# One Trainium2 core: the graph-attention walk in steps of two pairs, four of eight gathers made ahead, and coarser signals in the fill

## The reference

```
x += gat(layernorm(x))       # the part this case is about
x += moe_top1(layernorm(x))  # 8 experts, capacity 977
x += gcn2(layernorm(x))      # two graph convolutions over the same edges, with batch norm
x += moe_top2(layernorm(x))  # 8 experts, two per node

gat(h): feat = (h @ W) as [N, 4 heads, 64]
        el, er = <feat, attn_l>, <feat, attn_r> per head
        e = leaky_relu(el[src] + er[dst], 0.2)
        alpha = softmax of e over the edges of each dst
        out = elu(segment_sum(feat[src] * alpha, dst) + bias);  return h + out
```

## Time and profile before

| what | value |
|---|---|
| time, three runs | 7741.1 us median (7734.77 to 7762.5) |
| profiled execution: time, span | 7729.86 us, 7728.1 us |
| mean granted TensorE clock | 0.829 |
| busy: PE, PEld, DVE, ACT, POOL | 5449.5, 4407.3, 3508.0, 1732.1, 2142.1 us |
| fill: first and last product (line 607) | 327.7 and 2080.5 us |
| walk: first make_onehot (line 731) and last collect (line 772) | 2089.6 and 4025.1 us |
| indirect gathers (line 671) | 1664, busy 1674.6 us |

### The profile page before, as it was taken

How to read it: one execution, slowest core, us unless ns; L and a number is a source line. 1 busy time by engine, 2 the same in 40 slices (tenths; PEclk the granted TensorE clock), 3 DMA queues, 4 the chain that set the end, 5 groups by cost and what they waited for, 6 DMA issues and landing times. The chain is left out here.

```text
span 7728.1 us, 130980 instructions
## 1 busy us (share of the span) xinstructions
PE 5449.5 (71%) x37484; PEld 4407.3 (57%) x37485; DVE 3508.0 (45%) x10470; ACT 1732.1 (22%) x4193; POOL 2142.1 (28%) x2057
## 2 busy tenths in 40 slices
PE   2411115655577777777764995999969999549998
PEld 1200003333355555555543994888858888539997
DVE  5411117866666666666675555111161121532222
ACT  0200004666622222222222333000020000133332
POOL 2477770000055555555542220000000000052221
PEclk8655557877788888788875998999989999759999
DMA  3476661222244444444434662444402222336665
GB/s 119 121 212 195 193 202 58 92 86 98 101 116 116 118 116 116 116 115 116 117 91 135 177 177 75 157 152 157 158 26 102 96 95 92 121 136 181 183 180 169
DMA packets 448603, 1001.55 MB, mean 130 GB/s; under 512 B 56758, under 2 KB 314157, under 8 KB 428812
## 3 DMA queue, kind: packets, MB, share of 16 engines
q1 hardware_dynamic: 329116, 650.63, 26.1%
q0 software_dynamic: 112144, 268.88, 13.4%
q10 hardware_dynamic: 7200, 80.28, 2.5%
HBM read 713.64 MB, written 295.09 MB: 131 GB/s over the span
## 5 line engine op out<-in xcount | busy, mean ns | idle before, releaser
L671 POOL DMA_INDIRECT arena<-table,arena x1664 | 1674.6, 1006 | 2056.5 <-DVE arena L760 1623.9
L1249 PE MATMUL banks<-arena 128*128 128x256 bf16 x14700 | 1625.5, 273 | 25.5 <-DMA arena<-counts 25.5
L1249 PEld LDWEIGHTS banks<-arena 128*128 128x128 f16 x14700 | 1440.4, 98 | 206.7 <-DMA arena<-counts 26.3
L607 PE MATMUL banks<-arena 128*128 128x392 bf16 x2368 | 651.9, 436 | 1108.8 <-issue 718.8
L831 PE MATMUL banks<-arena 128*128 128x261 f32 x3328 | 1188.5, 489 | 162.0 <-DVE arena L760 81.3
L607 PEld LDWEIGHTS banks<-arena 128*128 128x128 bf16 x2368 | 350.1, 152 | 1410.1 <-issue 1373.4
L831 PEld LDWEIGHTS banks<-arena 128*128 128x128 f32 x3328 | 697.4, 233 | 276.4 <-DVE arena L760 93.6
L1868 POOL DMA_INDIRECT expert_in<-arena,slot x147 | 148.3, 1009 | 2306.2 <-DVEq L1809 2263.3
L1303 DVE TENSOR_TENSOR rings<-rings,banks 128x256 f32<-128x256 f32 x98 | 41.3, 421 | 1347.4 <-PE banks L1241 1347.4
L585 DVE TENSOR_TENSOR arena<-arena 128x1024 bf16<-128x1024 f16 x296 | 203.9, 689 | 988.5 <-remote 487.4
L2084 PEld LDWEIGHTS banks<-yt_ring,arena 128*128 128x128 f32 x5184 | 607.7, 193 | 15.4 <-DVE yt_ring L1973 4.1
(11 more groups left out here) (325 smaller groups left out, 5096.9 us busy)
## 6 DMA issues: line engine op xcount, KB each, us to landing
arena<-counts SPq DMA_DIRECT2D x100, 1568.0 KB, 6.6
arena<-in_L_ffn_W SPq DMA_DIRECT2D x114, 1024.0 KB, 5.2
edge_rows<-arena SPq DMA_DIRECT2D x312, 264.0 KB
arena<-edge_rows SPq DMA_DIRECT2D x312, 264.0 KB
counts<-arena ACTq DMA_DIRECT2D x50, 1568.0 KB, 5.1
arena<-in_L_ffn_w SPq DMA_DIRECT2D x64, 1024.0 KB
expert_in<-arena SPq DMA_DIRECT2D x25, 2028.0 KB
arena<-table,arena POOLq DMA_INDIRECT x1664
```

Source lines behind the costliest of these rows:

```text
L607: pe.matmul(psum_all[:, bass.ds(at_[p % 16], KEYS)], oh_b[:, p // LB % (OR // LB), :, p % LB], oh_k[:, p // KB % (OR // KB), :, p % KB], s ...
L671: pool.indirect_dma_start(out=got[:, u, j, :], out_offset=None, in_=table0, in_offset=bass.IndirectOffsetOnAxis(ap=src_sb[:, 2 * pair + j: ...
L1249: last = pe.matmul(psum[u][:, 0:D], a_ring[:, u, a, :], parts[:, a, k, :], start=(a == 0 and k == 0), stop=(a == NT - 1 and k == 2))
```

## The change

Everything is in the block described. In the fill, `hot` is raised every 8 steps instead of 4 and `done` every 4 instead of 1, with the numbers that others wait for scaled accordingly (`etab` is rounded up to whole groups of four); the number for `zeroed` now lies in the low bits of every fourth `ptab` entry, and TensorE takes it apart in registers instead of reading `ztab`. `KEPT` is 0, 1, 4, 5: four of eight, so that 416 pairs (832 gathers) are made ahead. The walk works on two pairs (q = 0 to 3) in each instruction where it can, and per q one signal takes the place of two. Per q TensorE does add_up(q), turn(q+3), spread(q+2); VectorE messages(q+1), score_sum(q+2), score_max(q+2), collect for the first pair, score_clamp(q+2), collect for the second, make_onehot(q+4); ScalarE copy_onehot(q+3), weights(q+2). A gather of q is four indirect DMAs behind one wait; a store or a load is one DMA of 512 rows. The diff, cut:

```diff
-KEPT = (0, 3, 6)
+KEPT = (0, 1, 4, 5)
+UQ = UN // 2
+KEPT_Q = tuple(u // 2 for u in KEPT[::2])
+LIVE_Q = tuple(u // 2 for u in LIVE[::2])
...
                     link(dve.tensor_scalar(ptab, ptab, 7, 9, ALU.bitwise_and, ALU.logical_shift_left))
+                    lead = ptab.rearrange("p (g u) -> p u g", u=PG)[:, 0, :]
+                    link(dve.tensor_tensor(lead, lead, ztab, ALU.add))
...
+                    link(dve.tensor_scalar(etab, etab, PG - 1, None, ALU.add))
+                    link(dve.tensor_scalar(etab, etab, PG.bit_length() - 1, None, ALU.arith_shift_right))
...
-                                    dve.wait_ge(done, p - OR + LB)
+                                    dve.wait_ge(done, (p - OR + LB) // PG)
...
-                                if p % PG == PG - KB:
+                                if p % LB == LB - KB:
                                     last.then_inc(hot, 1)
...
-                                need = load_many(mybir.EngineType.PE, ztab, p // PG, 16 // PG, 1, UNITS)
+                            bank = at_[p % 16]
                             if p % PG == 0:
-                                pe.wait_ge(zeroed, need[p % 16 // PG])
-                                pe.wait_ge(hot, p // PG + 1)
-                            pe.matmul(psum_all[:, bass.ds(at_[p % 16], KEYS)], oh_b[:, p // LB % (OR // LB), :, p % LB],
-                                      oh_k[:, p // KB % (OR // KB), :, p % KB],
-                                      start=False, stop=False, skip_group_check=True).then_inc(done, 1)
+                                need = pe.snap(bank & 511)
+                                bank = pe.snap(bank & (7 * 512))
+                                pe.wait_ge(zeroed, need)
+                                if p % LB == 0:
+                                    pe.wait_ge(hot, p // LB + 1)
...
+                            if p % PG == PG - 1:
+                                last.then_inc(done, 1)
...
+                weight = msg.rearrange("p (r u) j n -> p r (u j) n", r=2)
+                turned = onehot_t.rearrange("p (r u) j n -> p r (u j) n", r=2)
+                hot2 = onehot.rearrange("p (q u) j n -> p q (u j) n", q=UQ)
+                got2 = got.rearrange("p (q u) j n -> p q (u j) n", q=UQ)
+                banks_t = [psum[r] for r in range(2)]
+                banks_a = [[psum[4 + 2 * r + v] for v in range(2)] for r in range(2)]
...
                 def fetch_edges(pool):
-                        for n in range(NKEPT):
-                            i, u = divmod(n, UN)
-                            wait(pool, s_st[u], 16 * i)
-                            fetch(pool, u, n)
+                        for n in range(NKEPT // 2):
+                            i, q = divmod(n, UQ)
+                            wait(pool, s_st[q], 16 * i)
+                            fetch(pool, q, 2 * n)
                         for i in range(STEPS):
-                            for u in LIVE:
+                            for q in LIVE_Q:
                                 if i:
-                                    pool.wait_ge(s_m, UN * (i - 1) + u + 1)
+                                    pool.wait_ge(s_m, UQ * (i - 1) + q + 1)
...
                         def body(i):
-                            for u in range(UN):
-                                if u + 1 < UN or not final(i):
-                                    weights(i + (u + 1) // UN, (u + 1) % UN)
-                                if u + 3 < UN or not final(i):
-                                    copy_onehot(i + (u + 3) // UN, (u + 3) % UN)
+                            for q in range(UQ):
+                                three, two = later_(i, q, 3), later_(i, q, 2)
+                                if three:
+                                    copy_onehot(*three)
+                                if two:
+                                    weights(*two)
...
-                            for u in range(UN):
+                            for q in range(UQ):
-                                if two:
-                                    score_sum(*two)
+                                two, one = later_(i, q, 2), later_(i, q, 1)
                                 if one:
                                     messages(*one)
                                 if two:
+                                    score_sum(*two)
                                     score_max(*two)
-                                collect(i, u, tile(u))
+                                collect(i, q, 0, tile(2 * q))
                                 if two:
                                     score_clamp(*two)
+                                collect(i, q, 1, tile(2 * q + 1))
                                 if not final(i):
-                                    make_onehot(i + 1, u)
+                                    make_onehot(i + 1, q)
...
-                            for u in range(UN):
-                                add_up(i, u)
-                                if u + 4 < UN or not final(i):
-                                    turn(i + (u + 4) // UN, (u + 4) % UN)
-                                if u + 3 < UN or not final(i):
-                                    spread(i + (u + 3) // UN, (u + 3) % UN, tile(u))
+                            for q in range(UQ):
+                                three, two = later_(i, q, 3), later_(i, q, 2)
+                                add_up(i, q)
+                                if three:
+                                    turn(*three)
+                                if two:
+                                    spread(*two, lambda v: tile(2 * q + v))
```

More of the change, by code:

```diff
@@ L667, in tiles_of, with fetch @@
                     return lambda u: eng.snap((words[u // 4] // (1 << (6 * (u % 4)))) % 64)
-                def fetch(pool, u, pair):
-                        for j in range(2):
-                            pool.indirect_dma_start(out=got[:, u, j, :], out_offset=None, in_=table0,
+                def fetch(pool, q, pair):
+                        for j in range(4):
+                            pool.indirect_dma_start(out=got2[:, q, j, :], out_offset=None, in_=table0,
                                                     in_offset=bass.IndirectOffsetOnAxis(
@@ L785, in body @@
                             tile = tiles_of(dve, i, mybir.EngineType.DVE, tpack)
-                            for u in range(UN):
-                                two = (u + 2 < UN or not final(i)) and (i + (u + 2) // UN, (u + 2) % UN)
-                                one = (u + 1 < UN or not final(i)) and (i + (u + 1) // UN, (u + 1) % UN)
-                                if two:
-                                    score_sum(*two)
+                            for q in range(UQ):
+                                two, one = later_(i, q, 2), later_(i, q, 1)
                                 if one:
@@ L801, in walk_dve, with turn @@
                         steps(dve, body)
                 def walk_pe(pe):
-                        def turn(i, u):
-                            pe.wait_ge(s_oh, UN * i + u + 1)
-                            wait(pe, s_ht, UN * i + u - 1)
-                            for j in range(2):
-                                last = pe.matmul(banks_t[u][:, j * P:(j + 1) * P], onehot16[:, u, j, :, 1], ident16[:, :],
+                        def turn(i, q):
+                            pe.wait_ge(s_oh, UQ * i + q + 1)
+                            wait(pe, s_ht, UQ * i + q - 1)
+                            for j in range(4):
+                                last = pe.matmul(banks_t[q % 2][:, j * P:(j + 1) * P], hot2_16[:, q, j, :, 1], ident16[:, :],
@@ L823, in spread, with add_up @@
                             last.then_inc(s_b, 1)
-                        def add_up(i, u):
-                            n = UN * i + u
+                        def add_up(i, q):
+                            n = UQ * i + q
                             pe.wait_ge(s_m, n + 1)
-                            wait(pe, s_acc, n - RB + 1)
-                            for j in range(2):
-                                last = pe.matmul(banks_a[u][:, 0:mw], onehot[:, u, j, :], msg[:, u % RB, j, 0:mw],
-                                                 start=(j == 0), stop=(j == 1))
+                            wait(pe, s_acc, 2 * (n - 1))
+                            for v in range(2):
+                                for j in range(2):
+                                    last = pe.matmul(banks_a[q % 2][v][:, 0:mw], hot2[:, q, 2 * v + j, :],
+                                                     weight[:, q % 2, 2 * v + j, 0:mw], start=(j == 0), stop=(j == 1))
@@ L982, in _ @@
                         link(dve.tensor_copy(order[:, u, :], own_[:, k, :]))
[L983 removed]
+                for table, lo in ((tpack, 0), (tpack4, 4)):
                     four = trow2[:, lo:lo + PAIRS].rearrange("p (s u) -> p u s", u=4)
```

181 lines of the change are left out of this document (97 added, 84 removed).

## The result

Measured: 7811.5 us median against 7744.4 for the kernel before, ratio 1.0084 (95% interval 1.0071 to 1.0098): slower. Forecast were 7360 us and faster. The profiled execution has a span of 7812.4 us against 7728.1, +84.3.

What follows compares the result with a forecast made beforehand. Signals arriving late from TensorE beside the gathers were taken to bound the fill. 7729.9 − 247 (fill) − 10 (its end) + 1 (setup) − 121 (walk) = 7353, plus 11.2 to the median: 7364, said as 7360; range 7140 to 7840.

Steps and rivals of the forecast that it cites:

- The price of one signal: Fill beside the gathers: delay goes by signals, 2.80 us each; with two per block instead of eight, −247 us.
- the prediction's remark that the trace agrees in kind with a cost for each increment: Skill text puts increments after matmuls at 26.3 ns each, one after another; said to agree in kind, not size; unused.
- The first rival: Fill beside the gathers: TensorE's instructions carry the delay, blocks stay 22.4 us, total 7865; chance .18, without walk gain .04.
- its fill of +254 − 10: Under the first rival, the fill loses 254 us beside the gathers and gains 10 after them.
- its end at 1483: Slow part of the fill, 208 more gathers at 1.40 us, was to end at 1483 us instead of 1192.
- Gathers at 1.40: Gathers ahead in the fill: 624 took 293.9 to 1166.3, 1.40 us each; 208 more add 291 us.
- Signals after the gathers: End of the fill, after the gathers: coarser signals taken as −10 us, bounds −70 to +60.
- The walk: Walk on double pairs: 2.18 us a pair instead of 2.33, −121 us over 832 pairs; bounds −196 to +28.
- The step: Walk: a double step at the high clock taken as 3.0 us, from TensorE's 2.7 and two hand-overs of .2.
- VectorE's 2.78: Walk: VectorE's operations per double pair sum to 2.78 us against 3.24 before.
- the delay was priced per load: Walk: 1.05 us delay per load before, 1.4 per double-size load after; 3.85 us a round instead of 4.2.
- The range: Total time expected between 7140 and 7840 us, said to leave out about .18 of the chances.

Runs made afterwards that it cites:

- e2: Changed kernel with each product of the fill made by two matmuls (384 and 8 columns), same signals; 8002.7 us, one run.
- e1: Changed kernel with each partition's four rows one behind the other in edge_rows, for stores and loads; 7820.2 us, ratio 1.0051 to the kernel before.
- e3: Changed kernel without the stores of the kept rows, only one block stored and loaded again and again; 7822.9 us, one run.
- e7: Kernel before with the coarse signals of the fill alone, gathers and walk as before, on another chip; ratio 0.9945.
- e9: The changed kernel itself, unaltered, on another chip; 6819.6 us, ratio 1.0568 to the kernel before there.
- e11: Changed kernel with TensorE doing spread(q+2) ahead of turn(q+3), on another chip; 6523.4 us, ratio 1.0108 to the kernel before.
- e13: Changed kernel with spread ahead of turn and, on VectorE, a collect between sum and maximum and between maximum and clamp; 6406.1 us, ratio 0.9914 to the kernel before.
- e4: Changed kernel with two of eight pairs gathered ahead (KEPT 0, 1); 7649.8 us, ratio 0.9813 to the kernel before.
- e12: Changed kernel with two of eight pairs ahead and spread ahead of turn, on another chip; 6758.1 us, ratio 1.0464 to the kernel before.
- e15: Changed kernel with two of eight pairs ahead and both orders of the walk changed (TensorE's and VectorE's); 6806.8 us, ratio 1.0530 to the kernel before.
- e8: Changed kernel with nothing gathered ahead (KEPT empty), all 1664 gathers in the walk, on another chip; 7199.3 us, ratio 1.1152 to the kernel before.

## Why the prediction was wrong

*The price of one signal: the step that failed.* It read the .66 us between `collect` and the copy in the earlier trace rows as showing that the delay goes by signals, 2.80 each, and took 247 us off the fill. The changed kernel itself, with a quarter of the signals, keeps the block at 22.4 us, and e2, with the same two signals and twice the instructions, has 44.8. So the delay goes by instructions, 1.40 us each (or 2.80 for a product with its weight load), and the two signals of a block cost what eight did. What misled: a load's burst in the walk was taken for the same thing as the state beside the gathers ahead, because the packets per us agree (157 and 131). But in the earlier trace rows `collect` starts .36 us after the end of add_up, where in the slow part VectorE starts 40 us after the product it waits for. The row shows another state and can price nothing in this one, and e1 and e3 show that the stores' packets play no part in it. For the same reason the prediction's remark that the trace agrees in kind with a cost for each increment does not hold. The first rival was the true case; its fill of +254 − 10 stands against +239, and its blocks, its end at 1483 and its 104 steps in 291 us (108 by the windows) were met.

*Gathers at 1.40.* The end was right, 1456 us. But the stretch of 293.9 to 1166.3 holds 634 gathers, not 624, for the walk's first ten follow without a wait: 1.38 us each. In the changed kernel it is 840 up to 1456.13, 1.38 again, and as the walk's first eight are among them, the end came out.

*Signals after the gathers.* Taken −10; between step 480 and step 2360 VectorE's blocks took 825 us before and 805 after: −21. Within the bounds. On the other chips, where nothing is delayed, the coarse signals of the whole fill are worth the 38 us of e7.

*The walk.* −121 taken, −162 measured: the sign right, the working not. The step was put at 3.0 us by TensorE's 2.7 and VectorE's 2.78. Measured without anything held up it is 1694/416 = 4.07 (e9), since turn waits for the one-hot that VectorE makes last in its step, and spread and the score sum wait behind turn (e11: 3.37 without it). VectorE's 2.78 was too small besides: it priced sum, maximum and clamp as in the earlier trace rows, where `messages` lay between the sum and the maximum, while in the new order the maximum and both `collect` start .12, .20 and .27 us late (e11), and e13, which ends the first two, has 3.08. So the new walk is slower than the old where nothing is delayed (1694 against 1414). It is faster on the recorded chip because the old one loses 510 us there (1926) and the new one only 70 (1764), with half the signals and a step that has slack. Which of the two protects it, if either, was not separated: e11 and e13 ran on the other chips. That −162 lies near −121 is luck: the step behind it was put a third too short, and the delay was priced per load by its packets, while e1, whose loads lie in a quarter as many pieces, has the same walk (1762).

*The range* held the time, at its slow end, where it had been stretched over part of the first rival; the side was wrong, for the chances rested on one reading of one row.

## What to carry to other kernels

When two explanations fit a pitch equally (16 instructions or 8 signals in 22.4 us), a coincidence from another stage does not decide between them; the price must be shown in the stage itself, and both cases kept at nearly even chances. A test of that kind is e2: twice the instructions at equal signals. When operations are merged in a written-out order, recheck what stood between an operation and the one that needs its result, and which first item of a queue now waits for the other engine's last. And a kernel tuned on one chip should be timed on another: two of eight ahead was 2% faster on one (e4) and, with other orders in the walk, 5% slower on two others (e12, e15).

## What the runs showed of the hardware

- In the recorded runs and on the chip of e1 to e4 (the record does not say whether that is one chip), the engines that wait for TensorE's products in the fill learned of them late while GpSimd gathered back to back, and for 25 to 27 us after the last gather: VectorE started 39 to 40 us after the last product it needed, in e2 83.6, with eight signals in a block as with two. The pitch was 22.4 us for 8 products with 8 weight loads and 44.8 for 16 with 16. On the three other chips 2000 steps passed beside 620 gathers, and VectorE started at most 1.3 us after the product. The same program: 7779 against 6454 us. Why chips differ is open, and so is whether the delay belongs to the kernel or to the recording of its instructions, since every run here carries such a record. The Trainium skill, "SBUF — State Buffer", section "Who interferes with whom", gives TensorE read ports of its own and lets only VectorE and GpSimd get in each other's way. The rows show no such interference in VectorE either, whose operation of line 593 took .69 us beside the gathers and after them; no run here shows what delays the news of TensorE's products.
- An indirect gather of 128 rows of 1056 B took 1.36 to 1.47 us each in long rows that were not held back, the waits for a free slot included: 1.36 in the walk of e8, 1.40 ahead in e9, 1.42 in the walk of e12, 1.47 for the 416 ahead in e12.
- An operation of VectorE that needs the result of the one just before it, by a semaphore, started .03 us after that one's recorded end (the maximum in e11, 406 times); one held by nothing started .08 us before it.
